# A message-passing network over sorted edges: the read-back pass moved into layer 0, and PE's addresses worked out at the front of a step

## The chip, the cores and the metric

The kernel runs on one core of one Trainium2 chip. The metric is the device time of one launch, in microseconds (us). Engines are named as in the profile: PE does the matrix products, DVE, ACT and POOL do elementwise work, SP issues transfers (DMA), and every engine has a sequencer that fetches instructions, does its register work and waits for semaphores; the rows call it PEldq, SPq, POOLq.

## The reference

A graph of 3125 nodes with 64 features and 100000 edges sorted by destination, each with 16 attributes and one of 4 types. Three message steps, three relation layers, and a layernorm behind each half:

```python
# three times, with h = x at first
msg_in = concatenate([h[src], h[dst], edge_attr], axis=1)      # 100000 x 144
msg = silu(msg_in @ W1e + b1e) @ W2e + b2e
agg = segment_sum(msg, dst) / max(deg, 1)
h = h + silu(concatenate([h, agg], axis=1) @ W1n + b1n) @ W2n + b2n
x = layernorm(x + h)
# three times, with h = x at first; relu behind the first two
seg = edge_type * n_nodes + dst
agg = segment_sum(h[src], seg) / max(cnt, 1)                    # one mean for each node and type
h = h @ root + b + einsum('rni,rio->no', agg.reshape(4, n_nodes, 64), W)
x = layernorm(x + h)
```

## The kernel before

**Stages.** Nodes stand in 25 blocks of 128. A first stage (to about 1331 us) counts the edges by pair of blocks, gives every edge a slot, and scatters one record of 68 floats per edge to `recs` in DRAM: 64 with the edge's share of the message MLP, and four more, SRCLOC and PLACE (the local row of the source and of the destination), TYPE and PT (place and type in one number). Slots are in tiles of 128 records; a tile has one pair of source blocks. There are 1280 tiles in NG = 160 groups of GT = 8. Then come six layers over all groups, `l` = 0 to 2 the message steps and 3 to 5 the relation layers.

**The read-back pass** (L417 to L430 on SP, L668 to L675 on ACT, L875 to L883 on PE) stands between them. For each of the 160 groups SP loads its records, ACT copies their last four columns into `meta_t`, and SP may load again when a buffer of four is read. Then PE turns the columns SRCLOC and PLACE into rows, 20 transposes, ACT copies these, and SP stores them to `rows_d`. Layer 0 starts when this is stored.

**A group in layer 0.** SP loads the rows of the group, the same for all 128 partitions (`load_rows`, L433 to L437, two buffers `row_in`), and its records (`load_records`, L438 to L446, four buffers `rec_in`). DVE compares the rows with the partition's number, which gives three one-hot matrices for 8 tiles (`transposed_hots`, L1315 and L1316). They serve PE as gathers (`gather_tile`: per tile three products, L934, L935, L938, with parts of a table that holds the node terms in three bf16 parts), are turned for the sums (L948), and are stored to `hots_d` (`store_hots`, L451), from which layers 1 to 5 load them. DVE adds the gathered parts to the record (`messages`, L1337 and L1341, with the types' compare L1329), ACT does two silus (L701, L702), POOL splits the result in three bf16 parts with ACT's help (L537, L540, L707), PE sums it over the edges (`sum_messages`, L968, LAG = 3 groups later), ACT copies the sums out (L714) and POOL adds them to the block's total (L552 to L562). In layers 1 and 2 the one-hots come by DMA (`load_hots`), and the rest is the same.

**A group in layers 3 to 5.** PE gathers with two products a tile (L934, L935) and does 32 products of sums by type (L977), four behind each gathered tile. DVE makes the one-hots for those (`type_hots`, L1357) from a column of `meta_t`.

**Places.** Which 192 columns of the table a tile reads depends on the data: `load_places` (L913 to L918) loads the 8 offsets of the next group, in layers 0 to 2 the destination's offset too, from `places` in SBUF into registers of PE's sequencer. `stage` (L982 to L1011) takes a snapshot of the registers (L988, L990), waits for the one-hots, and works out each address just ahead of its product. In layers 0 to 2 `load_places(g + 1)` stands behind the sums, at the step's end; in layers 3 to 5 in mid-step, behind the fourth tile.

**What sets the order.** The program is written out by hand. Each engine has one stream, four groups a loop pass, and waits for the others' semaphores; a semaphore is counted up once for each group, `done(n)` being group n's count. On SP a step of layer 0 is: load rows k, load records k, store one-hots k - 2. On ACT it is keep_hots (L693), middle (L707), keep_msums (L714), messages (L701). On DVE it is the one-hots of the next group, then the additions of this one.

## Time and profile before

| what | value |
|---|---|
| time, median of 3 runs | 5863.55 us (5863.24 to 5865.77) |
| the profiled execution: its time, its span | 5864.59 us, 5862.9 us |
| mean granted clock of TensorE | 0.863 |
| PE busy | 4725.5 us (81%), 47638 instructions |
| PE's weight loads busy | 4058.5 us (69%) |
| DVE busy | 3972.5 us (68%), 9658 instructions |
| POOL busy | 3395.9 us (58%) |
| ACT busy | 2755.2 us (47%) |
| DMA | 975.41 MB in 358467 packets, mean 166 GB/s |
| chain that ended last | PE 56%, POOL 15%, issue 10%, DMA 9%, DVE 7% |

The shares are averages over stages that have different limits, so they say little about one change; the rows below are read stage by stage. The chain is followed back from the last instruction to whatever released each step; "issue" is time in which an engine waited for nothing that the profile shows. The ends of products on PE are modelled (a product shows some 0.25 us busy while they start 0.08 us apart), so PE's pace is read from the starts. The stages by time: first stage to 1331 us, read-back pass to 1511, layer 0 from 1516 to 2312, layers 1 and 2 with their node steps to about 3750, layers 3 to 5 to the end.

### The profile page before, as it was taken

The numbers are of one execution on the slowest core, as the hardware profiler recorded it, in microseconds if no ns is written. First come the engines' busy times: TensorE is split into PE (matmuls) and PEld (weight loads), VectorE is DVE, ScalarE is ACT, GpSimd is POOL, SyncE is SP. The second block draws the span as 40 slices with busy tenths as digits, with TensorE's granted clock in tenths as the row PEclk, the third lists the DMA queues.
The fourth block names the chain that finished last, engine by engine and source line by source line (L and its number), as shares of the span: only waits on it lengthen the run. The fifth ranks groups of instructions, "written<-read, shape, count | busy, mean of one in ns | idle before, by whom it ended". The sixth has DMA issues, their size and how long they took to land.

```text
span 5862.9 us, 173813 instructions
## 1 busy us (share of the span) xinstructions
PE 4725.5 (81%) x47638; PEld 4058.5 (69%) x47639; DVE 3972.5 (68%) x9658; ACT 2755.2 (47%) x4407; POOL 3395.9 (58%) x4499
## 2 busy tenths in 40 slices
PE   2666666660577777888888888899999999999998
PEld 2444444440466665777767777699998999999997
DVE  6444444440589997777767777688875888578885
ACT  1111111112456665677757777555554555455553
POOL 0777777770367775455535555366653666446663
PEclk9755555555799999999999999899998999899997
DMA  8111111117899997777757777244432444234441
GB/s 327 29 29 29 29 29 29 29 28 244 272 312 333 334 334 245 248 264 266 264 176 265 263 265 265 92 133 133 132 120 83 132 132 133 93 109 133 132 133 58
DMA packets 358467, 975.41 MB, mean 166 GB/s; under 512 B 71168, under 2 KB 83796, under 8 KB 358411
## 3 DMA queue, kind: packets, MB, share of 16 engines
q1 hardware_dynamic: 317352, 946.00, 48.9%
q0 software_dynamic: 38400, 28.13, 2.7%
q10 hardware_dynamic: 2658, 0.51, 0.0%
q8 instruction: 37, 0.61, 0.0%
q14 instruction: 20, 0.16, 0.0%
HBM read 774.54 MB, written 199.06 MB: 166 GB/s over the span
## 4 chain that ended last, share of the span: by engine, by line
PE 56%; POOL 15%; issue 10%; DMA 9%; DVE 7%; another core or an unknown queue 2%; ACT 1%; DVEq 0%; POOLq 0%; SPq 0%; ACTq 0%
PE sums L977 21%; POOL recs L517 14%; PE gat L934 10%; PE gat L935 10%; DMA arena<-rows_d 5%; PE gat L938 4%; PE sums L968 4%; DMA arena<-recs 3%; PE sums L948 2%; DMA recs<-arena 2%; DVE arena L1341 1%; PE gat L1060 1%; DVE arena L1316 1%; DVE arena L1337 1%
## 5 line engine op out<-in xcount | busy, mean ns | idle before, releaser
L934 PE MATMUL gat<-table,arena 128*128 x7680 | 1913.4, 249 | 370.8 <-DVE arena L1341 186.7
L935 PE MATMUL gat<-table,arena 128*128 x7680 | 1916.7, 250 | 0.0
L977 PE MATMUL sums<-arena 128*128 128x192 bf16 x15360 | 1887.2, 246 | 0.0
L1357 DVE TENSOR_SCALAR arena<-iota_s,meta_t 128x512 bf16<-128x512 int16 x3840 | 1523.0, 469 | 363.2 <-PE sums L977 363.2
L977 PEld LDWEIGHTS sums<-arena 128*128 128x128 bf16 x15360 | 1325.3, 98 | 0.1
L517 POOL DMA_INDIRECT recs<-arena x800 | 949.8, 1187 | 377.4 <-issue 374.9
L721 ACT CAST arena<-gat 128x768 bf16<-128x768 f32 x960 | 767.0, 799 | 809.3 <-PE gat L935 809.3
L934 PEld LDWEIGHTS gat<-table,arena 128*128 128x128 bf16 x7680 | 747.7, 97 | 548.3 <-issue 482.1
L938 PE MATMUL gat<-table,arena 128*128 x3840 | 959.9, 250 | 0.0
L540 POOL TENSOR_TENSOR arena<-arena 128x512 bf16<-128x512 f32 x480 | 532.6, 1110 | 726.3 <-ACT arena L707 726.0
L1341 DVE TENSOR_TENSOR arena<-arena,gat 128x256 f32<-128x256 f32 x1920 | 812.0, 423 | 65.8
L935 PEld LDWEIGHTS gat<-table,arena 128*128 128x128 bf16 x7680 | 748.0, 97 | 137.2 <-issue 0.4
L592 POOL TENSOR_TENSOR arena<-arena 128x256 f32<-128x256 f32 x480 | 414.5, 864 | 656.7 <-ACT arena L729 655.9
L693 ACT COPY arena<-sums 128x1024 bf16<-128x1024 bf16 x480 | 486.3, 1013 | 518.2 <-PE sums L948 517.8
L1337 DVE TENSOR_TENSOR arena<-gat,arena 128x256 f32<-128x256 f32 x960 | 402.8, 420 | 263.4 <-PE gat L938 262.1
L832 PE MATMUL gat<-arena 25*125 25x39 bf16 x800 | 232.0, 290 | 401.8 <-DVE arena L1179 401.8
L656 ACT COPY arena<-gat 25x1000 bf16<-25x1000 bf16 x100 | 98.4, 984 | 829.8 <-PE gat L806 807.8
L832 PEld LDWEIGHTS gat<-arena 25*125 25x125 bf16 x800 | 141.2, 176 | 445.9 <-DVE arena L1179 429.7
L598 POOL TENSOR_TENSOR arena<-arena 128x256 f32 x480 | 384.6, 801 | 91.2 <-POOL arena L595 91.2
L968 PE MATMUL sums<-arena 128*128 128x192 bf16 (+1 forms) x3840 | 406.1, 248 | 11.1 <-ACT arena L714 10.9
L729 ACT COPY arena<-sums 128x768 f32<-128x768 f32 x480 | 386.2, 804 | 9.9 <-PE sums L977 9.9
L938 PEld LDWEIGHTS gat<-table,arena 128*128 128x128 bf16 x3840 | 380.3, 99 | 13.4
(184 smaller groups left out, 6228.6 us busy)
## 6 DMA issues: line engine op xcount, KB each, us to landing
arena<-hots_d SPq DMA_DIRECT2D x320, 768.0 KB, 4.5
arena<-hots_d SPq DMA_DIRECT2D x480, 512.0 KB, 3.5
arena<-recs SPq DMA_DIRECT2D x640, 272.0 KB, 3.9
hots_d<-arena SPq DMA_DIRECT2D x160, 768.0 KB, 8.1
arena<-rows_d SPq DMA_DIRECT2D x160, 512.0 KB, 6.9
recs<-arena SPq DMA_DIRECT2D x1, 43520.0 KB, 119.4
recs<-arena POOLq DMA_INDIRECT x800, 2.9
arena<-in_edge_attr_dram SPq DMA_DIRECT2D x100, 62.5 KB
```

What stands on the lines that cost most here:

```text
L517: pool.indirect_dma_start(recs, bass.IndirectOffsetOnAxis(ap=addr_out[s][:, j:j + 1].bitcast(U32), axis=0), rec_out[s][:, j, :], None).the ...
L540: pool.tensor_tensor(parts[u][:, :, 2 * HID:K3], left[s], parts[u][:, :, HID:2 * HID], ALU.subtract).then_inc(low_made, 1)
L693: act.copy(oh[u], oh_ps[u % 2].rearrange("p (j n) -> p j n", n=P)).then_inc(hot_out, 1)
L721: act.copy(gb[u % 4][:, 4 * h:4 * h + 4, :], gat[:, 1024 * h:1024 * h + 1024].rearrange("p (j w) -> p j w", j=4) [:, :, 0:K3]).then_inc(ga ...
L934: pe.matmul(at, ohT[u][:, 0, tile], table_flat[:, bass.ds(off[j], K3)], start=True, stop=False)
L935: ins = pe.matmul(at, ohT[u][:, 1, tile], table_next[:, bass.ds(off[j], K3)], start=False, stop=l >= LAYERS)
L938: ins = pe.matmul(at, ohT[u][:, 2, tile], table_flat[:, bass.ds(dst_off, K3)], start=False, stop=True)
L968: ins = pe.matmul(accp[u % 2][:, 0:w], oh[u][:, j, :], parts[u][:, j, 0:w], start=j == 0, stop=j == GT - 1)
L977: ins = pe.matmul(accp[s][:, 256 * r:256 * r + K3], oh4[u][:, t, r * P:(r + 1) * P], gb[u][:, t, :], start=t == 0, stop=t == GT - 1)
L1337: dve.tensor_tensor(z[s][:, tiles, :], found_parts[:, tiles, 0:HID], rec[:, tiles, 0:HID], ALU.add).then_inc(z_step, 1)
L1341: ins = dve.tensor_tensor(z[s][:, tiles, :], z[s][:, tiles, :], found_parts[:, tiles, m * HID:(m + 1) * HID], ALU.add)
L1357: ins = dve.tensor_scalar(oh4[u][:, j, :], iota_s[:], meta_t[:, bass.ds(GT * g + j, 1), PT - HID], None, ALU.is_equal)
```

## The change

- **The read-back pass is gone.** In layer 0 SP loads each group's records six groups ahead (`load_first`, eight buffers `rec_in` in place of four). PE turns their columns SRCLOC and PLACE into 8 rows each, two transposes a group, four groups ahead (`turn_rows`); ACT copies them to `rows_sb` (`keep_rows`, three groups ahead), SP stores them to `rows_d` (`store_rows`, three ahead), waits for that store, and loads them for all partitions (`load_rows`, two ahead). `rows_d` now has the 16 rows of a group side by side, so that a partition reads 4 KB in one piece.
- **`meta_t` is replaced by `place_type`**, one column in place of four, which ACT copies from the records of each group in layer 0 (`keep_types`) and DVE reads in layers 3 to 5.
- **Loops.** Layer 0 runs eight groups a loop pass on every engine, the other layers four as before. The number of groups stays 160.
- **The front of a step on PE**, in all six layers: behind the snapshot, the addresses of all the step's products are worked out at once (`lower_ap`), and in layers 0 to 2 `load_places(g + 1)` follows there, ahead of the wait for the one-hots, in place of standing behind the sums.
- POOL's wait ahead of layer 0 is for the scatters themselves.

```diff
-    NG += -NG % 4
+    NG += -NG % 8
...
-    rows_d = nc.dram_tensor("rows_d", [2, NT, P], BF16, kind="Internal").ap()
+    rows_d = nc.dram_tensor("rows_d", [NG, 2 * GT, P], BF16, kind="Internal").ap()
...
+    rows_by_group = rows_d.rearrange("g (m j) p -> j g m p", m=2)
+    rows_flat = rows_d.rearrange("g r p -> g (r p)")
 
...
-        meta_t = sb("meta_t", [P, NT, 4])
+        place_type = sb("place_type", [P, NT])
...
-            with sp.Fori(0, QUADS) as i:
-                for u in range(4):
-                    sp.wait_ge(meta_kept, done(4 * i + u - 4))
-                    sp.dma_start(rec_in[u].rearrange("p j w -> p (j w)"),
-                                 recs_by_group[:, bass.ds(4 * i + u, 1), :].rearrange("p a w -> p (a w)")
-                                 ).then_inc(meta_loaded[u], 16)
-            sp.wait_ge(rows_cast, TP // 2)
-            for m in range(2):
-                sp.dma_start(rows_d[m].rearrange("(c q) p -> q c p", q=P), rows_sb[:, m, :, :]
-                             ).then_inc(rows_stored, 16)
-            sp.wait_ge(meta_kept, done(NG - 1))
-            sp.wait_ge(rows_stored, 32)
-
-            def load_rows(k, u):
+            def load_first(k, u):
+
+                if not isinstance(k, int) or k >= 8:
+                    sp.wait_ge(gat_read, done(2 * (k - 8) + 1))
+                    sp.sem_inc(recs_go, 1)
+                    sp.wait_ge(type_kept, done(k - 8))
+                sp.dma_start(rec_in[u].rearrange("p j w -> p (j w)"),
+                             recs_by_group[:, bass.ds(k, 1), :].rearrange("p a w -> p (a w)")
+                             ).then_inc(rec_loaded[u], 16)
+
+            def store_rows(k, u):
+
+                sp.wait_ge(rows_cast, k + 1)
+                sp.sem_inc(rows_go, 1)
+                sp.dma_start(rows_by_group[:, bass.ds(k, 1), :, :].rearrange("j a m p -> j (a m) p"), rows_sb[u % 2]
+                             ).then_inc(rows_stored[u % 2], 16)
+
+            def load_rows(k, u, i):
+                sp.wait_ge(rows_stored[u % 2], 16 * (k // 2 + 1) if isinstance(k, int) else 64 * i + 16 * (u // 2 + 1))
+                sp.sem_inc(rows_go, 1)
                 sp.wait_ge(ohT_made, done(k - 2))
                 sp.sem_inc(rows_go, 1)
-                sp.dma_start(row_in[u % 2], rows_by_group[:, bass.ds(k, 1), :].rearrange("m a e -> a m e")
-                             .to_broadcast([P, 2, GT * P])).then_inc(rows_loaded[u % 2], 16)
+                sp.dma_start(row_in[u % 2].rearrange("p m e -> p (m e)"),
+                             rows_flat[bass.ds(k, 1), :].to_broadcast([P, 2 * GT * P])).then_inc(rows_loaded[u % 2], 16)
...
+            def first_layer(k, u, i):
+                known = isinstance(k, int)
+                if not known or k + 6 < NG:
+                    load_first(k + 6, (u + 6) % 8)
+                if not known or k + 3 < NG:
+                    store_rows(k + 3, u + 3)
+                if not known or k + 2 < NG:
+                    load_rows(k + 2, u + 2, i)
+                if not known or k >= 1:
+                    store_hots(k - 1, u + 7)
+
+            for k in range(6):
+                load_first(k, k)
+            for k in range(3):
+                store_rows(k, k)
+            for k in range(2):
+                load_rows(k, k, 0)
+            for k in range(8):
+                first_layer(k, k, 0)
+            with sp.Fori(1, OCTS - 1) as i:
+                for u in range(8):
+                    first_layer(8 * i + u, u, i)
+            for k in range(NG - 8, NG):
+                first_layer(k, k % 8, 0)
+            store_hots(NG - 1, 3)
...
+            def keep_rows(k, u, i):
+                act.wait_ge(rows_turned, k + 1)
+                act.wait_ge(summed, done(k - 7))
+                if not isinstance(k, int):
+                    act.wait_ge(rows_stored[u % 2], 64 * i + 16 * (u // 2))
+                elif k >= 2:
+                    act.wait_ge(rows_stored[u % 2], 16 * (k // 2))
+                act.copy(rows_sb[u % 2], rows_ps[(u + 1) % 2]).then_inc(rows_cast, 1)
+
+            def keep_types(k, u, i):
+                act.wait_ge(rec_loaded[u % 8], 16 * (k // 8 + 1) if isinstance(k, int) else 16 * i + 16)
+                act.copy(place_type[:, bass.ds(GT * k, GT)], rec_in[u % 8][:, :, PT]).then_inc(type_kept, 1)
...
+                    def group(g, u, i, l=l):
+                        known = isinstance(g, int)
+                        if l == 0 and (not known or g + 3 < NG):
+                            keep_rows(g + 3, u + 3, i)
+                        keep_hots(g, u % 4)
+                        if not known or g >= 1:
+                            middle(g - 1, (u + 3) % 4)
+                        if not known or g >= 4:
+                            keep_msums(g - 4, u % 4)
+                        if l == 0:
+                            keep_types(g, u, i)
+                        messages(g, u % 4)
+
...
-            pe.wait_ge(meta_kept, done(NG - 1))
-            for r in range(TP // 2):
-                if r >= 4:
-                    pe.wait_ge(rows_cast, r - 3)
-                for a in range(4):
-                    m, c = divmod(4 * r + a, TP)
-                    ins = pe.transpose(work[r % 4][:, a * P:(a + 1) * P], meta_t[:, c * P:(c + 1) * P, m], ident[:])
+            def turn_rows(k, u, i):
+
+                pe.wait_ge(rec_loaded[u % 8], 16 * (k // 8 + 1) if isinstance(k, int) else 16 * i + 16 * (1 + u // 8))
+                if not isinstance(k, int) or k >= 2:
+                    pe.wait_ge(rows_cast, k - 1)
+                pe.wait_ge(acc_read, done(k - 9))
+                for m in range(2):
+                    ins = pe.transpose(rows_ps[(u + 1) % 2][:, m, :], rec_in[u % 8][:, :, SRCLOC + m], ident[:])
                 ins.then_inc(rows_turned, 1)
...
                         off = [pe.snap(r, min_val=0, max_val=SPAN * ROWW * (NS - 1)) for r in tile_regs[u % 2]]
                         if l < LAYERS:
                             dst_off = pe.snap(dst_reg[u % 2], min_val=0, max_val=ROWW * (NB - 1) + K3)
+                            pe.lower_ap(table_flat[:, bass.ds(dst_off, K3)])
+                        for r in off:
+                            pe.lower_ap(table_flat[:, bass.ds(r, K3)])
+                            pe.lower_ap(table_next[:, bass.ds(r, K3)])
+                        if l < LAYERS:
+                            load_places(g + 1, u + 1)
                         gather_ready(g, u, i)
                     if l < LAYERS:
                         if gathers:
                             for j in range(GT):
                                 gather_tile(g, u, j, off, dst_off)
-                            turn_dst_hots(g, u)
+                            turn_dst_hots(g, u % 4)
+                        if l == 0 and (not known or g + 4 < NG):
+                            turn_rows(g + 4, u + 4, i)
                         if not known or g >= LAG:
                             sum_messages(g - LAG, (u + 4 - LAG) % 4)
-                        if gathers:
-                            load_places(g + 1, u + 1)
...
-                    stage(g, g, 0)
-                with pe.Fori(1, QUADS) as i:
-                    for u in range(4):
-                        stage(4 * i + u, u, i)
+                if l == 0:
+                    for k in range(4):
+                        turn_rows(k, k, 0)
+                    for g in range(8):
+                        stage(g, g, 0)
+                    with pe.Fori(1, OCTS - 1) as i:
+                        for u in range(8):
+                            stage(8 * i + u, u, i)
+                    for g in range(NG - 8, NG):
+                        stage(g, g % 8, 0)
...
                         ins = dve.tensor_scalar(oh4[u][:, j, :], iota_s[:],
-                                                meta_t[:, bass.ds(GT * g + j, 1), PT - HID], None, ALU.is_equal)
+                                                place_type[:, bass.ds(GT * g + j, 1)], None, ALU.is_equal)
```

How this moves instructions shows in three places. First PE, layer 1, from the sums that end a step to the first gathers of the next; "ISA" is register work of the sequencer (snapshot, addresses). Before:

```order
L968 MATMUL sums<-arena 128x192 [waits low_made,hot_out]
L968 MATMUL sums<-arena 128x192 x7
L916 ISA
L916 TENSOR_LOAD places
L988 ISA
L931 ISA [waits hots_loaded1]
L934 ISA [waits gat_read]
L934 MATMUL gat<-table,arena 128x192
L935 ISA
L935 MATMUL gat<-table,arena 128x192
```
and now:

```order
L1012 MATMUL sums<-arena 128x192 [waits low_made,hot_out]
L1012 MATMUL sums<-arena 128x192 x7
L1032 ISA
L1035 ISA
L1038 ISA
L1037 ISA x2
L1038 ISA x3
L960 ISA
L960 TENSOR_LOAD places
L975 ISA [waits hots_loaded1]
L978 MATMUL gat<-table,arena 128x192 [waits gat_read]
L979 MATMUL gat<-table,arena 128x192
```
The load of places is now behind the snapshot (L1032) and behind the entries that work out the addresses (L1035 to L1038), and the entries between the gathers are gone.

Second PE in layer 3, between the last sums of one step and the first of the next. Before:

```order
L977 MATMUL sums<-arena 128x192 x4
L988 ISA
L931 ISA [waits hots_loaded1]
L934 ISA [waits gat_read]
L934 MATMUL gat<-table,arena 128x192
L935 ISA
L935 MATMUL gat<-table,arena 128x192
L954 REGISTER_ALU
L961 REGISTER_ALU [waits acc_read]
L977 MATMUL sums<-arena 128x192 [waits gat_read,oh_made]
```
and now:

```order
L1021 MATMUL sums<-arena 128x192 x4
L1032 ISA
L1037 ISA
L1038 ISA x3
L1037 ISA x2
L1038 ISA
L975 ISA [waits hots_loaded3]
L978 MATMUL gat<-table,arena 128x192 [waits gat_read]
L979 MATMUL gat<-table,arena 128x192
L998 REGISTER_ALU
L1005 REGISTER_ALU [waits acc_read]
L1021 MATMUL sums<-arena 128x192 [waits gat_read,oh_made]
```
Here no load of places moves; seven entries with all addresses (L1037, L1038) come between the snapshot and the wait for the one-hots, and those ahead of single gathers are gone.

Third SP, one group of layer 0. Before:

```order
L433 REGISTER_ALU
L435 ISA [waits ohT_made]
L435 DMA arena<-rows_d 128x2x1024
L440 ISA
L444 ISA [waits gat_read,types_made]
L444 DMA arena<-recs 128x544
L451 ISA [waits ohT_made]
L451 DMA hots_d<-arena 128x3072
```
and now (L429 loads records six groups ahead, L437 stores the rows of the group three ahead, L445 loads those of the group two ahead):

```order
L426 ISA
L429 ISA [waits gat_read,type_kept]
L429 DMA arena<-recs 128x544
L437 ISA [waits rows_cast]
L437 DMA rows_d<-arena 8x2x128
L443 REGISTER_ALU [waits rows_stored1]
L445 DMA arena<-rows_d 128x2048 [waits ohT_made]
L459 ISA [waits ohT_made]
L459 DMA hots_d<-arena 128x3072
```
The load of rows has moved behind two more waits, those for the cast rows and for their store, and the store of the one-hots is for the group before in place of the one two before.

## Rows read from the trace of the kernel before

**Rows 1.** The page's busy tenths in 40 equal slices, PE's row.
```profile
PE   2666666660577777888888888899999999999998
```

**Rows 2.** Chain of waits, 1325 to 1512 us: start, us, what.
```profile
1328.49 2.99 DMA recs<-arena
...
1333.72 3.67 DMA arena<-recs
...
1501.28 4.53 PE gat L881 x20
```

**Rows 3.** Timeline, 1495 to 1531 us: start, us, engine, line, operation, out<-in, [idle before].
```profile
1516.65 0.88 DVE L1315 TENSOR_SCALAR arena<-arena,lane 128x1024 bf16<-128x1024 bf16 x2 [192.99 <-DMA arena<-rows_d]
...
1527.55 0.88 DVE L1341 TENSOR_TENSOR arena<-arena,gat 128x256 f32<-128x256 f32 x2
...
1529.08 0.61 ACT L702 ACTIVATE arena<-arena 128x512 bf16<-128x512 f32 x1
```

**Rows 4.** Stages: us, then PE, PEld, DVE, ACT, POOL busy, PEclk, DMA share, GB/s.
```profile
1512.00:1762.00 250.00, 181.61 (x1879) 150.61 (x1880) 201.94 (x476) 138.17 (x231) 159.56 (x264) 0.92 0.94 307
1762.00:2312.00 550.00, 410.84 (x4524) 335.23 (x4522) 514.67 (x1132) 328.97 (x570) 395.45 (x698) 0.98 0.96 331
2350.00:3005.00 655.00, 572.40 (x6400) 463.63 (x6400) 494.19 (x1121) 457.28 (x800) 363.49 (x640) 0.99 0.78 260
```

**Rows 5.** Groups by line, layer 0 (1512 to 2312 us): busy, mean ns, idle before.
```profile
L1315 DVE TENSOR_SCALAR arena<-arena,lane 128x1024 bf16<-128x1024 bf16 x320 | 190.8, 638 | 237.2 <-DMA arena<-rows_d 233.6 <-issue 0.2
...
L714 ACT COPY arena<-sums 128x196 f32<-128x196 f32 x160 | 51.0, 319 | 3.2 <-POOL arena L562 3.2
```

**Rows 6.** DMA issues, 1505 to 1530 us: KB each, median us to landing.
```profile
rows_d<-arena SPq DMA_DIRECT2D x2, 320.0 KB, 3.5
```

**Rows 7.** DMA issues, layer 1, 2400 to 2800 us.
```profile
arena<-hots_d SPq DMA_DIRECT2D x99, 768.0 KB, 4.5
```

**Rows 8.** The load of rows, L435, by line, 1505 to 1600 us.
```profile
DMA to landing us min/median/max: 5.7/8.2/9.6
```

**Rows 9.** Timeline in layer 0, 2004 to 2007 us, DVE and SP.
```profile
2004.28 1.32 DVE L1316 TENSOR_SCALAR arena<-arena,lane 128x1024 bf16<-128x1024 bf16 x1
...
2005.85 0.39 SPq L435 DMA_DIRECT2D arena<-rows_d  x1
...
2006.67 0.33 SPq L444 DMA_DIRECT2D arena<-recs  x1
```

**Rows 10.** Timeline of PE in layer 1, 2599.9 to 2604.3 us.
```profile
2600.19 0.25 PE L934 MATMUL gat<-table,arena 128*128 x1 [0.38 <-issue]
...
2602.44 0.61 PE L948 MATMUL sums<-ident_b,arena 128*128 128x128 bf16 x8
2602.89 0.83 PE L968 MATMUL sums<-arena 128*128 128x192 bf16 x8
2603.97 0.25 PE L934 MATMUL gat<-table,arena 128*128 x1 [0.25 <-issue]
```

**Rows 11.** L916 on PE's sequencer, 2602 to 2604 us: min/median/max ns, starts.
```profile
L916 PEldq FUSED_REGOPS  x1: 65/65/65, 2602.5 to 2602.5; - x1
L916 PEldq TENSOR_LOAD <-places x1: 836/836/836, 2602.7 to 2602.7; - x1
```

**Rows 12.** The snapshot L988 in layer 3, 4005 to 4006 us.
```profile
L988 PEldq FUSED_REGOPS  x1: 150/150/150, 4005.4 to 4005.4; - x1
```

**Rows 13.** Timeline of PE in layer 3, 4006 to 4007.5 us.
```profile
4006.84 0.25 PE L934 MATMUL gat<-table,arena 128*128 x1
```

**Rows 14.** Sequencer entries of other lines: L582 in layer 3, others in layer 1.
```profile
L582 POOLq FUSED_REGOPS  x6: 84/84/84, 4010.4 to 4089.6; - x6
...
L1016 PEldq COMPARE_BRANCH  x24: 207/208/208, 2414.3 to 2784.6; - x24
...
L988 PEldq FUSED_REGOPS  x75: 165/165/165, 2402.7 to 2796.7; - x75
...
L934 PEldq FUSED_REGOPS  x796: 37/37/42, 2400.2 to 2799.1; - x199
```

More of the change, by code:

```diff
@@ L204, in gnn_kernel @@
         loops_at = at
-        for s in range(4):
+        for s in range(8):
             t, at = carve(at, GT * REC)
@@ L211, in gnn_kernel @@
         macc_v = macc.rearrange("p (b w) -> p b w", b=NB)
+        rows_sb = []
+        for s in range(2):
+            t, at = carve(at, P, BF16, GT)
+            rows_sb.append(t.rearrange("j (m p) -> j m p", m=2))
         rings_at = at
@@ L267, in gnn_kernel @@
         oh_ps = [sums[:, 1024 * s + 512:1024 * s + 1024].bitcast(BF16) for s in range(2)]
+        rows_ps = [sums[0:GT, 1024 * s + 256:1024 * s + 512].rearrange("j (m p) -> j m p", m=2) for s in range(2)]
         hot_turned = gat[:, 0:512].bitcast(BF16)
@@ L347, in gnn_kernel @@
         stored = sem("stored")
-        rec_loaded = [sem(f"rec_loaded{s}") for s in range(4)]
+        rec_loaded = [sem(f"rec_loaded{s}") for s in range(8)]
         rows_loaded = [sem(f"rows_loaded{s}") for s in range(2)]
@@ L519, in _ @@
                             rec_out[s][:, j, :], None).then_inc(rec_stored[s], 16)
-            pool.wait_ge(meta_kept, done(NG - 1))
+            for s in range(2):
+                pool.wait_ge(rec_stored[s], 16 * GT * (EG // 2))
             pool.wait_ge(tables_in, 32)
```

113 lines of the change are left out of this document (50 added, 63 removed).

## The prediction

> **What bounds the kernel now.** I read the busy table by slices first, then the busy time of each engine by stage, then the chain of waits stage by stage, and last single steps in the timeline. PE's row of slices shows three regimes: a hole in the tenth slice, sevens and eights, then nines [rows 1]. The hole is the pass that the change takes away. The chain goes from the last scatter of records from 1333.72 through 160 loads of records to 20 transposes at 1501.28 [rows 2], then through the store of the rows and their first load; nothing else runs, and the first one-hot compare of layer 0 starts at 1516.65 [rows 3]. The scatter landed at 1328.49 + 2.99 = 1331.48, so the pass and the start after it cost 185.2 us.
>
> Layer 0 runs 160 groups from 1516.65 to 2312, 795 us, or 4.97 a group. DVE is busy (201.9 + 514.7)/160 = 4.48 of that, and the DMA rings 0.94 to 0.96 of the time [rows 4]. DVE sat idle 233.6 us before its first compare, waiting for the rows [rows 5]. So this layer has two masters: a loop "rows land, one-hots are made, the next load into that buffer starts", and DVE itself. In layers 1 and 2 PE sets the pace: 6400 matmuls in 655 us, 40 a group, 4.09 us a group [rows 4]. In layers 3 to 5 it runs back to back, 48 matmuls a group: the nines at the end of its row [rows 1].
>
> **The pass goes.** What starts layer 0 now is a chain for group 0 alone: load of records 3.7 [rows 2], two transposes and a copy about 1.1, store of its rows 3.5 [rows 6], load of rows 5.7 [rows 8], issues between them 1.3, and 1.6 for standing among five more loads of records: 16.9 us in place of 185.2. That is **-168**.
>
> **The loop of the row loads gets longer.** Before, the load of rows k+2 starts 0.25 us after the one-hots of k are done: L1316 ends at 2005.60, the issue is at 2005.85 [rows 9]. In the changed order on SP it stands behind the store of rows k+3. That waits for ACT's copy of rows k+3, which stands on ACT behind the messages of group k-1. These wait for DVE's additions of group k-1, and on DVE those come after the one-hots of k, which wait for rows k. So from landing k to issue k+2:
> - DVE, one-hots of k and additions of k-1: 4.4 (4.48 on average; a little less when POOL is less busy);
> - ACT, two silus: from 1528.43 (1527.55 + 0.88) to 1529.69, 1.26 [rows 3];
> - the copy of 256 columns with its waits, 0.42 (196 columns take 0.32 [rows 5]);
> - SP: 0.25 to the issue of the store, and 0.82 from that to the next issue with its two waits, as between the issues at 2005.85 and 2006.67 [rows 9]: 1.07.
>
> Together 7.15 us. Then the load lands after L. The loop spans two groups, since there are two row buffers, so a group takes (7.15 + L)/2. L is 5.7 at least, 8.2 at the median when DMA is full [rows 8]. After the change DMA has gaps (4.97 of work in more than 6 us), and a row of 4 KB in place of two of 2 KB may help; 768 KB landed in 4.5 where the rings were 0.78 busy [rows 4, 7]. I take 5.3, which gives 6.22 a group. Bounds: 3.9 gives 5.5 a group, 7.3 gives 7.2. The cost is (6.22 - 4.97) x 160 = **+200**; the bounds are +90 and +360. The additions on PE (two transposes of 4.53/20 = 0.23 [rows 2]) and ACT (a copy of 8 columns, less than 0.32) fall into time that this loop leaves idle, and cost nothing; if the loop were shorter than 5 us they would be late next. Bytes are the same but for 4 KB a group.
>
> By the Trainium skill ("DMA: Bandwidth & Descriptors", section "Anatomy of one DMA") a transfer takes about 2 us plus its bytes over 436 GB/s, 3.2 us for these 512 KB. The trace has 5.7 for the first one, with almost nothing ahead of it; by the rule the layer would cost 168 us less.
>
> **The front of the step on PE, layers 1 and 2.** PE's sequencer handles register work in order, and what it has sent ahead to PE hides it. Before, at a plain step: the address of the places at 2602.5 (65 ns), a load of nine registers 836 ns, then one entry of 165 ns and two short ones like the 37 ns of L934 [rows 10, 11, 14]. With 0.06 between entries that is the 1.45 us from there to the gather at 2603.97. At 2602.5 PE had 5 of its 8 transposes and all 8 sums before it; the last sum started near 2603.47, half a us before the next gather. Now the same stretch holds the snapshot (165 ns), seven entries of about six operations, the address and the load of places, and the wait. An entry of six operations takes 84 ns on POOL [rows 14]. So 0.22 + 7 x 0.14 + 0.12 + 0.90 + 0.10 + 0.03 = 2.35 us.
>
> How far ahead can the sequencer be? In layer 3 the snapshot starts at 4005.4, and the next step's first gather on PE at 4006.84 - 0.08 for the weight load: 1.4 us, 17 matmuls of 0.082 [rows 12, 13]. It could send faster: a tile's entries take it 0.25 us, its six matmuls 0.49. So this lead is a cap. In layers 1 and 2 the last 17 matmuls are 8 sums of 0.082, 8 transposes of 0.056 and one gather: 1.18 us. So 2.35 - 1.18 = 1.17 stay open. In return the gathers run without register entries, at 0.082: 24 x 0.082 + 8 x 0.056 + 8 x 0.082 = 3.07, in place of 3.3. A plain step becomes 4.24; before it was 3.78 (2600.19 to 2603.97) [rows 10]. Every fourth carries the branch (208 ns [rows 14], its counter and gaps) and one more entry, 0.12 a group on average; filling the layer adds 0.05. So 4.41 against 4.09: 320 groups, **+102**. The bounds: nothing of the front visible, and the next limit is the ring DVE additions, two silus, DVE's remainder, 3.5 us: -0.5 a group, -160; a load that is as slow as in layer 0 would give +0.5 more, which I think not likely here.
>
> **Layers 3 to 5.** The load of places stays in mid-step. The front is the snapshot, six such entries, a shorter one and the wait: 0.22 + 6 x 0.14 + 0.10 + 0.10 + 0.03 = 1.29 us against a lead of 1.39, so it is just covered. Behind it stand three waits of 0.09 each between the first gathers (0.165 of work) and the first sums, with no lead left: 0.05 open. At the branch the front is 1.68, so 0.29 + 0.15 are open. On average 0.14 a group, 480 groups: **+68**. Bounds: 0, and 0.35 a group (+170).
>
> **Sum.** -168 + 200 + 102 + 68 = +202 on the profiled execution's 5864.59 (its span of 5862.9 and 1.7 around it); the median of the runs is 5863.55, 1 us away. Forecast 6067 us.
>
> **Rivals.**
> - *The sequencer's lead is longer than I read it* (ends faster). If it covers 2.35 us in layers 1 and 2, PE loses nothing there, and a group drops to about 3.6 us: -0.45 x 320 = -144, layers 3 to 5 at 0. Sum -168 + 200 - 144 = -112: 5753. For it: in layers 1 and 2 no step shows more than 13 matmuls sent, so no cap was met there. Against it: the constant 1.4 us in layer 3 [rows 12, 13]. It decides from 2.35 us of lead, twice what I see. The Trainium skill ("TensorE: Matmul & The Clock Gate", "Architectural detail") gives TensorE a queue of 64; counted as 32 weight loads with their matmuls it would reach far enough in those layers. The trace stops at 17.
> - *The rows land quickly* (L 3.9, fronts as forecast): 5.5 a group, -168 + 90 + 102 + 68 = +92: 5957.
> - *The front costs and gives nothing*, the loop as forecast: +32: 5897.
> - *The change doesn't lengthen the loop*, because ACT's copy is ready earlier than I read: layer 0 keeps 4.97, -168 + 170 = +2: 5867. Against it is the order on ACT, which is fixed.
>
> **How the numbers follow.** Forecast 0.50 (own range 5990 to 6200), longer lead 0.17, quick rows 0.15, neutral front 0.10, unchanged loop 0.08. What a measurement of this kernel can tell from no change is 0.2%, 12 us. Slower: 0.50 + 0.15, 0.08 of the neutral front and 0.02 of the unchanged loop, 0.75. Faster: 0.17, 0.02 of the neutral front and 0.03 of the unchanged loop, 0.22. Same: the rest of the unchanged loop, 0.03. The range 5800 to 6240 leaves out the longer lead for the most part, and the tail above.
>
> **What would show each step.** The first one-hot compare near 1348. In layer 0, a group near 6.2 us, with the load of rows issued about 1 us after ACT's copy and DVE idle some 1.7 us a group before its first compare, waiting for rows. In layers 1 and 2, 4.4 us a group, gathers 0.082 apart, and a hole of about 1.2 us on PE before each step's first gather, put down to issue. In layers 3 to 5, a hole of 0.3 to 0.4 at every fourth step. I am wrong if layers 1 and 2 take under 3.9 a group, or if the loads of rows are issued before ACT's silus of their step.

## The result

The changed kernel takes 6041.06 us (median of 4 runs, 6040.43 to 6042.81) against 5864.45 in the same comparison: a ratio of 1.0302, 95% interval 1.0284 to 1.0319. The profiled execution has a span of 6039.2 us against 5862.9, so 176.3 us are to be explained; its mean granted clock is 0.862 against 0.863, so the clock is not the reason. Single executions of two kernels below were over 1.5% longer than the fastest of the same kernel (6110.9 against 5978.1 us with the front alone, 5714.4 against 5496.0 us with the last combination), and the ratios leave them out. The stages, from the starts of the first one-hot compare and of the first and last gather of each layer in both traces ("a group" is the time from first to last gather over 160):

| stage | before us | after us | difference | forecast |
|---|---|---|---|---|
| first one-hot of layer 0 at | 1516.65 | 1344.99 | -171.7 | -168 |
| layer 0, from there to its last gather (a group) | 778.7 (4.86) | 1007.7 (6.29) | +229.0 | +200 |
| layer 1, first to last gather (a group) | 641.6 (4.010) | 677.6 (4.235) | +36.0 | +51 |
| layer 2 | 641.5 | 678.1 | +36.6 | +51 |
| layer 3 (a group) | 631.4 (3.946) | 644.3 (4.027) | +12.9 | +23 |
| layer 4, layer 5 | 631.2, 631.4 | 643.9, 643.8 | +12.7, +12.4 | +45 |
| between and behind the layers | 390.5 | 398.8 | +8.3 | 0 |
| sum | | | +176.3 | +202 |

The page of the changed kernel, PE's slices [rows 1] and, below them, the granted clock and the DMA share:

```profile
PE   2666666656666666777777777799999999999998
...
PEclk9555555568888887999999999899997999899997
DMA  8111111127777775777747777344442444334441
```

The hole in PE's tenth slice is gone. Layer 0 now fills eight slices (the ninth to the sixteenth), a five and seven sixes where five sevens stood, and DMA, nines before in layer 0, shows sevens. The first compare, in the timeline, answers to [rows 3]:

```profile
1344.99 0.88 DVE L1376 TENSOR_SCALAR arena<-arena,lane 128x1024 bf16<-128x1024 bf16 x2 [20.23 <-DMA arena<-rows_d]
```

The stages, layer 0 in two and layer 1, answer to [rows 4] (us, then PE, PEld, DVE, ACT, POOL busy, PEclk, DMA share, GB/s):

```profile
1345.00:1595.00 250.00, 162.31 (x1614) 148.80 (x1614) 170.77 (x393) 123.23 (x264) 126.31 (x211) 0.87 0.73 246
1595.00:2350.00 755.00, 499.01 (x5022) 454.93 (x5023) 536.22 (x1197) 386.70 (x837) 418.12 (x716) 0.89 0.75 253
2415.00:3085.00 670.00, 514.38 (x6294) 478.78 (x6293) 481.14 (x1105) 457.00 (x785) 311.95 (x616) 1.00 0.74 250
```

In layer 0 every engine is less busy than in [rows 4], DMA too: no engine is full, so a loop of waits must set the pace. The compare of the rows by form, layer 0, for [rows 5]:

```profile
L1376 DVE TENSOR_SCALAR arena<-arena,lane 128x1024 bf16<-128x1024 bf16 x320 | 202.6, 673 | 282.2 <-DMA arena<-rows_d 282.2
```

and the load of rows from issue to landing, by line, for [rows 8]:

```profile
DMA to landing us min/median/max: 4.2/5.7/6.3
```

DVE waits 282.2 us for rows, of which 20.23 lie ahead of the first compare. Before it was 233.6, of which 192.99 lay ahead of the first: the wait within the layer went from 41 to 262 us. Two groups of layer 0 in the timeline show the loop, for [rows 9]:

```profile
1904.13 0.61 ACT L727 ACTIVATE arena<-arena 128x512 bf16<-128x512 f32 x1
...
1904.65 0.34 ACT L697 CAST arena<-sums 8x256 bf16<-8x256 f32 x1
...
1904.95 1.71 DVE L1376 TENSOR_SCALAR arena<-arena,lane 128x1024 bf16<-128x1024 bf16 x2 [1.39 <-DMA arena<-rows_d]
...
1905.26 0.31 SPq L437 DMA_DIRECT2D rows_d<-arena  x1
...
1906.07 0.35 SPq L445 DMA_DIRECT2D arena<-rows_d  x1
...
1906.59 0.47 DVE L1377 TENSOR_SCALAR arena<-arena,lane 128x1024 bf16<-128x1024 bf16 x1
...
1910.48 0.63 ACT L727 ACTIVATE arena<-arena 128x512 bf16<-128x512 f32 x1
1911.00 0.34 ACT L697 CAST arena<-sums 8x256 bf16<-8x256 f32 x1
...
1911.58 0.31 SPq L437 DMA_DIRECT2D rows_d<-arena  x1
...
1912.21 0.35 SPq L445 DMA_DIRECT2D arena<-rows_d  x1
```

The second silu (L727) ends at 1904.74, the cast of the rows (L697) at 1904.99, the store (L437) is issued at 1905.26 and the load of rows (L445) 0.81 later. The one-hots of group k start at 1904.95 with the landing of its rows; the load for k + 2 is issued at 1912.21, 7.26 us later, though its buffer was read at 1907.06. PE in layer 1, timeline, for [rows 10]:

```profile
2600.15 0.61 PE L992 MATMUL sums<-ident_b,arena 128*128 128x128 bf16 x8
2600.60 0.83 PE L1012 MATMUL sums<-arena 128*128 128x192 bf16 x8
2602.31 0.25 PE L978 MATMUL gat<-table,arena 128*128 x1 [0.88 <-issue]
...
2604.30 0.61 PE L992 MATMUL sums<-ident_b,arena 128*128 128x128 bf16 x8
2604.75 0.83 PE L1012 MATMUL sums<-arena 128*128 128x192 bf16 x8
2606.48 0.25 PE L978 MATMUL gat<-table,arena 128*128 x1 [0.90 <-issue]
```

The load of places there, by line (min/median/max ns), for [rows 11]:

```profile
L960 PEldq FUSED_REGOPS  x1: 60/60/60, 2601.2 to 2601.2; - x1
L960 PEldq TENSOR_LOAD <-places x1: 841/841/841, 2601.3 to 2601.3; - x1
```

and the packed entries of the addresses (L1038), by line, for [rows 14]:

```profile
L1038 PEldq FUSED_REGOPS  x280: 74/74/74, 2502.3 to 2796.8; - x140
```

Gathers come 0.082 apart now (24 of them from 2602.31 to 2604.30), and ahead of the first there is a hole that the profile puts down to issue. The snapshot, which starts at 2600.01, and what is behind it take until 2602.31. Counted over the trace, 17 products start between a snapshot (L1032) and the first gather that comes of it, at 587 of 590 snapshots in layers 1 to 5, and never more. In layer 3 only the step with the branch has holes; in the timeline of PE, for [rows 13]:

```profile
4106.56 0.49 PE L1021 MATMUL sums<-arena 128*128 128x192 bf16 x4
4107.06 0.25 PE L978 MATMUL gat<-table,arena 128*128 x1
4107.15 0.25 PE L979 MATMUL gat<-table,arena 128*128 x1
4107.38 0.42 PE L1021 MATMUL sums<-arena 128*128 128x192 bf16 x3
```

The four sums from 4106.56 should be followed by the gather at 4106.89; it comes 0.17 late, and the sum at 4107.38 another 0.15. Before the change no two starts in layers 3 to 5 are over 0.083 apart, their first 20 and last 5 us left out.

### The profile page after: what moved, and what is told of

The parts are those of the page before. It is cut to its first block, busy times and chain, and to the rows that moved or that the text cites. A ratio compares the mean times of both kernels' runs of the same rounds, so it can differ in the third digit from the quotient of the medians.

```text
span 6039.2 us, 164954 instructions
## 1 busy us (share of the span) xinstructions
PE 4743.4 (79%) x47938; PEld 4219.4 (70%) x47939; DVE 3961.0 (66%) x9658; ACT 2783.2 (46%) x4562; POOL 3312.6 (55%) x4499
## 4 chain that ended last, share of the span: by engine, by line
PE 52%; DVE 9%; issue 7%; DMA 7%; ACT 2%; POOL 1%; SPq 1%; DVEq 0%; POOLq 0%; ACTq 0%
PE sums L1021 21%; PE gat L978 10%; PE gat L979 9%; DMA arena<-rows_d 6%; PE gat L982 3%; DVE arena L1406 3%; PE sums L1012 3%; PE sums L992 2%; DVE arena L1402 2%; PE gat L1121 1%; DVE arena L1415 1%; PE gat L1119 1%; ACT arena L727 1%; DVE arena L1377 1%; DVE arena L1376 1%
## 5 line engine op out<-in xcount | busy, mean ns | idle before, releaser
L978 PE MATMUL gat<-table,arena 128*128 x7680 | 1940.3, 253 | 691.0 <-issue 370.1
L979 PE MATMUL gat<-table,arena 128*128 x7680 | 1937.6, 253 | 0.0
L1422 DVE TENSOR_SCALAR arena<-iota_s,place_type 128x512 bf16<-128x512 int16 x3840 | 1523.7, 469 | 403.1 <-PE sums L1021 403.1
L978 PEld LDWEIGHTS gat<-table,arena 128*128 128x128 bf16 x7680 | 770.0, 100 | 832.9 <-issue 482.9
L982 PE MATMUL gat<-table,arena 128*128 x3840 | 990.8, 258 | 0.0
L979 PEld LDWEIGHTS gat<-table,arena 128*128 128x128 bf16 x7680 | 772.2, 101 | 3.7
L982 PEld LDWEIGHTS gat<-table,arena 128*128 128x128 bf16 x3840 | 395.8, 103 | 3.7
```

The costliest lines, as they stand in the source:

```text
L978: pe.matmul(at, ohT[u % 4][:, 0, tile], table_flat[:, bass.ds(off[j], K3)], start=True, stop=False)
L979: ins = pe.matmul(at, ohT[u % 4][:, 1, tile], table_next[:, bass.ds(off[j], K3)], start=False, stop=l >= LAYERS)
L982: ins = pe.matmul(at, ohT[u % 4][:, 2, tile], table_flat[:, bass.ds(dst_off, K3)], start=False, stop=True)
L1422: ins = dve.tensor_scalar(oh4[u][:, j, :], iota_s[:], place_type[:, bass.ds(GT * g + j, 1)], None, ALU.is_equal)
```

## Experiments

Twelve kernels in three sets. "us a group" is again the time from first to last gather of a layer in the profiled execution, over 160.

**The front alone.** The kernel before, with `lower_ap` for all addresses and `load_places` behind the snapshot, as in the second hunk of the change:

```diff
+                            pe.lower_ap(table_flat[:, bass.ds(dst_off, K3)])
+                        for r in off:
+                            pe.lower_ap(table_flat[:, bass.ds(r, K3)])
+                            pe.lower_ap(table_next[:, bass.ds(r, K3)])
+                        if l < LAYERS:
+                            load_places(g + 1, u + 1)
...
-                        if gathers:
-                            load_places(g + 1, u + 1)
```


> The kernel before with nothing changed but the front of the step on PE, in all six layers (addresses worked out at once, the load of places ahead of the wait for the one-hots). Theory (the front is register work that the sequencer can hide only behind 17 matmuls): layers 1 and 2 go from 4.01 to 4.24 us a group, layers 3 to 5 from 3.946 to 4.025, as in the changed kernel, +73 and +38; layer 0 keeps its time, since DVE and the rows set its pace. About 5864 + 111 = 5975. Rival (the layers 1 to 5 became slower through the other edits, such as the narrower column for the type compare or the records' buffers): within 10 us of 5864. Second rival: the front also shows in layer 0, up to +50 more, 6025.

Measured: 4.235 us a group in layers 1 and 2, 4.02 to 4.05 in layers 3 to 5, within 0.003 of the changed kernel but for layer 3 with 4.047. Its times spread: 5978.1, 5980.5, 6042.3 and 6110.9, ratio 1.0241 (1.0185 to 1.0297). The lower two agree with 5975, the mean of the lower three is 6000. The profiled execution is the longest, with 906 us in layer 0 against 778 before; there DVE waits 106.6 us for gathers in 122 groups, which is the second rival's picture. The executions do not agree on it, so what the front costs in layer 0 of this kernel, and why one execution pays it and another does not, stays open. That the front makes layers 1 to 5 slower is shown.

**The front taken out.** The changed kernel with those lines the other way round, in all layers.

> The changed kernel with PE's front of the step put back as it was before in all six layers; the read-back in layer 0 stays. Theory: layers 1 to 5 return to 4.01 and 3.946 us a group, layer 0 stays at 6.29: 6041 - 111 = 5930. Rival (a part of layer 0's loss is PE's longer front): layer 0 at 5.9 or less, below 5870.

Measured: 5896.47 us, ratio 1.0066 (1.0049 to 1.0083). Layers 1 to 5 are back at 4.01 and 3.945. Layer 0 went to 985.6 us, 22 less than in the changed kernel: the front has a price in layer 0 that I had set at nothing, though a tenth of the layer's loss and not the rival's part. 207 us remain there with the read-back and SP's order alone, where I forecast 200.

**Two issues exchanged on SP.**

```diff
+                if not known or k + 2 < NG:
+                    load_rows(k + 2, u + 2, i)
                 if not known or k + 3 < NG:
                     store_rows(k + 3, u + 3)
-                if not known or k + 2 < NG:
-                    load_rows(k + 2, u + 2, i)
```


> The changed kernel with two issues on SP exchanged in layer 0: the load of rows k+2 ahead of the store of rows k+3. Theory (the loop of two row buffers runs through the additions, the silus and the cast because the load stands behind the store): that loop is cut. What is left is the store itself, which now has to land before the load of the next step: one-hots k done, 2.6 additions, 1.26 silus, 0.42 copy, 0.25 issue, 3.5 landing, 0.3 issue, 5.3 landing over three groups, 1.8 for the one-hots, 15.4 over three groups: 5.1 us a group, 6041 - 185 = 5856. Rival (the time from issue to landing of the rows, or DMA traffic as such, sets layer 0): 6.2 to 6.3 us a group, 6041 within 15 us.

Measured: 5854.74 us, ratio 0.9991 (0.9981 to 1.0001), layer 0 at 5.126 us a group. So 186 us of layer 0's loss hang on this order: the loop is shown. The number was hit by luck, for the wrong reason. Groups by line on DVE, 1400 to 2100 us:

```profile
L1377 DVE TENSOR_SCALAR arena<-arena,lane 128x1024 bf16<-128x1024 bf16 x136 | 161.1, 1185 | 0.0
...
L1376 DVE TENSOR_SCALAR arena<-arena,lane 128x1024 bf16<-128x1024 bf16 x272 | 136.6, 544 | 5.7 <-issue 4.2 <-DMA arena<-rows_d 1.6
...
L1402 DVE TENSOR_TENSOR arena<-gat,arena 128x256 f32<-128x256 f32 x272 | 114.8, 422 | 34.8 <-PE gat L982 31.7
```

DVE hardly waits for rows any more (1.6 us in 136 groups); it would if the store's landing were the limit. It is busy 4.7 us a group and waits for gathers (31.7), which points to the front of the step; the last combination below tries that.

**One more group of lead.** The exchange, and 7, 5, 4 and 4 groups of lead in place of 6, 4, 3 and 3 for the load of records, the turn, the cast and the store.

> As the kernel with the two issues exchanged, and turning, casting, storing and loading of records each one group further ahead (5, 4, 4 and 7 groups). Theory: the store has a whole group more to land, and layer 0 is at the pace that it had before or a little better, 4.5 to 4.9 us a group (DVE is busy 4.48 of it): 6041 - 229 to - 285, 5756 to 5812. If it is no faster than with the exchange alone, the store's landing was not what was left.

Measured: 5925.22 us, ratio 1.0112 (1.0095 to 1.0129), 5.54 us a group: slower by 70 than the exchange alone, a miss. DVE waits for rows again, by the same view (DVE's line numbers are one higher in this kernel and the next, so L1377 here is the pair of compares that was L1376):

```profile
L1377 DVE TENSOR_SCALAR arena<-arena,lane 128x1024 bf16<-128x1024 bf16 x252 | 147.4, 626 | 126.7 <-DMA arena<-rows_d 126.3 <-issue 0.2
...
L1403 DVE TENSOR_TENSOR arena<-gat,arena 128x256 f32<-128x256 f32 x250 | 104.0, 416 | 7.0 <-PE gat L983 7.0
```

With 8 buffers and 7 groups of lead the load of records waits for the additions of the group before, and the load of rows stood behind it. The next kernel tests that.

```diff
+                if not known or k + 2 < NG:
+                    load_rows(k + 2, u + 2, i)
                 if not known or k + 7 < NG:
                     load_first(k + 7, (u + 7) % 8)
-                if not known or k + 2 < NG:
-                    load_rows(k + 2, u + 2, i)
```


> As the kernel with the two issues exchanged and all read-back work one group further ahead, and with the load of rows k+2 as the first issue of the step, ahead of the load of records k+7 too. Theory of why the one without this came to 5.54 us a group: with a lead of 7 groups over 8 buffers the load of records k+7 waits for the additions and the type copy of group k-1, and the load of rows stood behind that wait. Then layer 0 falls to DVE's pace with its contention, 4.71 us busy a group: 4.75 to 5.0 a group, 5785 to 5830 in all. Rival (the longer lead itself costs, by DMA or by the copies on ACT): 5.4 us a group or more, 5900.

Measured: 5896.25 us, ratio 1.0059 (1.0042 to 1.0076), 5.37 us a group.

```profile
L1377 DVE TENSOR_SCALAR arena<-arena,lane 128x1024 bf16<-128x1024 bf16 x256 | 126.6, 537 | 4.2 <-issue 3.9 <-DMA arena<-rows_d 0.2
...
L1403 DVE TENSOR_TENSOR arena<-gat,arena 128x256 f32<-128x256 f32 x258 | 108.8, 422 | 82.1 <-PE gat L983 81.1
```

The wait for rows went from 126.3 to 0.2 us, so its cause is shown; the time followed only in part, since DVE now waits 81.1 us for gathers. The longer lead bought nothing: 5.37 us a group against 5.126 without it, as the rival had it. Why it makes the gathers later was not tried.

**The load of places in mid-step.** The changed kernel:

```diff
-                        if l < LAYERS:
-                            load_places(g + 1, u + 1)
...
                                 gather_tile(g, u, j, off, dst_off)
+                                if j == 3:
+                                    load_places(g + 1, u + 1)
```


> The changed kernel with one edit: in layers 0 to 2 the load of places for the next group stands behind the fourth gathered tile, where it stands in layers 3 to 5, and not at the front of the step. All addresses are still worked out at the front. Theory (a front of 2.30 us against a lead of 1.25 leaves the hole of 1.05; the load with its address is 1.0 of it): the hole in layers 1 and 2 all but closes, the load is hidden behind the gathers, and the next limit is DVE's ring with the silus, about 3.5 us a group in place of 4.24: -235. Layer 0 gives back the 22 us that the front cost it. 6041 - 257 = 5784. Rival (the hole is set by something else that comes with the step, such as the one-hots' landing or the wait for DVE): layers 1 and 2 stay at 4.2, about 6020.

Measured: 5759.97 us, ratio 0.9832 (0.9816 to 0.9848). Layers 1 and 2 at 3.45 us a group: with the load gone from the front, a group is 0.79 us shorter, and the layers are faster than before the change. PE in layer 1:

```profile
2603.96 0.25 PE L982 MATMUL gat<-table,arena 128*128 x1
2604.28 0.25 PE L978 MATMUL gat<-table,arena 128*128 x1
...
2605.28 0.61 PE L992 MATMUL sums<-ident_b,arena 128*128 128x128 bf16 x8
2605.72 0.83 PE L1012 MATMUL sums<-arena 128*128 128x192 bf16 x8
2606.43 0.25 PE L978 MATMUL gat<-table,arena 128*128 x1
```

The hole ahead of the step is 0.05 us (the last sum ends its 0.082 at 2606.38), and behind the fourth tile 0.24 opens. A plain step is 3.29 to 3.38, one with the branch 3.77. Layer 0 gave back 28 us. Whether 3.45 is DVE's ring, as I had expected, is not shown.

The same place for the load, but each address ahead of its product:

> The changed kernel without any address worked out at the front, in all six layers (each is worked out ahead of its product, as before), and in layers 0 to 2 with the load of places behind the fourth gathered tile. Theory: the front is only the snapshot and the wait, the gathers of a step take 2.25 us in place of 1.97, and the load of 0.84 costs a little of the lead that is left: about 3.6 us a group in layers 1 and 2, -205; layers 3 to 5 back to 3.946, -38; layer 0 gives back 22. 6041 - 265 = 5776. If it is clearly faster or slower than the kernel with addresses in front and the load in mid-step, the packing of addresses has a price or a gain of its own in layers 1 and 2.

Measured: 5904.47 us, ratio 1.0075 (1.0058 to 1.0092): layers 1 and 2 at 4.012, where I had expected 3.6. PE, layer 1:

```profile
2602.17 0.25 PE L979 MATMUL gat<-table,arena 128*128 x1
2602.25 0.25 PE L982 MATMUL gat<-table,arena 128*128 x1
2603.21 0.25 PE L978 MATMUL gat<-table,arena 128*128 x1 [0.71 <-issue]
2603.34 0.25 PE L979 MATMUL gat<-table,arena 128*128 x1
```

The hole has only moved, behind the fourth tile. 4.012 is also the pace of the kernel before, with the load at the end. So in both it is the sequencer's whole work that sets the step, 4.0 us: 17 entries of addresses that start 0.12 us apart are 2.0, the load with its address 1.0, the snapshot 0.23, and the rest goes to waits and the branch. The trace of the kernel before bears this out: in the step from 2599.99 to 2603.77 no two entries of the sequencer have more than 0.1 us between them. Seven packed entries at 0.133 take 0.93. The gain needs the packing (4.012 without it, 3.45 with it, both with the load in mid-step), and the load behind it at the front was the loss. Packed addresses with the load at the step's end were not tried.

**Together.** First the load of rows first, the longer lead, and the plain addresses with the load in mid-step:

> The kernel with the load of rows first and the longer lead, together with the front put back and the load of places in mid-step in layers 0 to 2. The parts lie in different layers and should add: layer 0 4.75 to 5.0 us a group, layers 1 and 2 3.6, layers 3 to 5 3.946: 5787 - 205 - 38 = 5545 or a little more, some 5% below the kernel before.

Measured: 5706.41 us, ratio 0.9739 (0.9722 to 0.9755). 161 above the expectation: 132 are the 4.01 of layers 1 and 2 in place of 3.6, the rest is layer 0 at 4.93, where 5545 had stood for 4.75.

Then with packed addresses in layers 0 to 2 only, once with the longer lead, once with the changed kernel's leads and just the exchange:

> The last combination with one difference: in layers 0 to 2 the addresses are worked out at the front of the step and the load of places stands behind the fourth gathered tile (3.45 us a group in layers 1 and 2 with that, against 4.01 with each address ahead of its product); layers 3 to 5 keep the address ahead of each product (3.946). Theory: the parts add, layer 0 stays at DVE's and DMA's pace, 4.9 us a group: 5706 - 0.56 x 320 = 5527. Rival (the front costs in layer 0, where DVE waits for gathers): layer 0 at 5.1 or more, 5555 or more.

> As the last combination with the packed addresses, but with the leads of the changed kernel (6, 4, 3 and 3 groups) and only the two issues exchanged. Theory: the store of the rows must land within a step here, and it does at 5.1 us a group but not much below; layer 0 at 5.0 to 5.1, 5540 to 5560. If it is as fast as the kernel with longer leads, the exchange alone was all that the loop needed.

Measured: 5514.03 us, ratio 0.9404 (0.9389 to 0.9420), and 5497.15 us, ratio 0.9377 (0.9359 to 0.9396). Layer 0 at 4.84 and 4.74, layers 1 and 2 at 3.44, layers 3 to 5 at 3.946. The last kernel is the fastest. It disproves what I expected of the store: it keeps the short lead and is the faster one. It also shows what was left with the exchange alone, since in layer 0 it differs from that kernel only in the place of the load of places: DVE's wait for gathers is gone, and layer 0 went from 5.126 to 4.74 us a group. Its DVE in layer 0:

```profile
L1376 DVE TENSOR_SCALAR arena<-arena,lane 128x1024 bf16<-128x1024 bf16 x296 | 238.7, 846 | 15.5 <-DMA arena<-rows_d 11.4 <-issue 4.0
...
L1402 DVE TENSOR_TENSOR arena<-gat,arena 128x256 f32<-128x256 f32 x295 | 122.8, 416 | 0.0
```

**The front edit on the kernel before, done this way.**

> The kernel before with one edit: in layers 0 to 2 the addresses are worked out at the front of the step, and the load of places stands behind the fourth gathered tile. The read-back pass stays, layers 3 to 5 as before. Theory (in layers 1 and 2 PE's sequencer is the bound, and packed entries take it less time): 3.45 in place of 4.01 us a group, -180, layer 0 within 20 of its time: 5682. Rival (the gain belongs to the changed kernel's other edits): 5860.

Measured: 5688.49 us, ratio 0.9699 (0.9682 to 0.9715), 3.45 us a group in layers 1 and 2, layer 0 within 3 us of its time. The gain belongs to the packed addresses with the load in mid-step and needs nothing else of the change.

**Pieces of 2 KB in place of 4 KB.** The changed kernel with `rows_d` as [2, NT, P], and the load of rows with two pieces a partition.

> The changed kernel with the rows of a group in DRAM as in the kernel before: two pieces of 2 KB for a partition in place of one of 4 KB. All else, the order on SP too, as changed. Theory (half of the landing time goes into the group in layer 0, and larger pieces land faster): landing 6.2 or more in place of 5.6 us, layer 0 at 6.55 or more in place of 6.29 us a group, 6080 or more. Rival (the size of the pieces does not matter where DMA has gaps): 6041 within 10.

Measured: 6056.73 us, ratio 1.0331 (1.0314 to 1.0349); layer 0 at 6.378. DMA issues, 1400 to 2300 us (KB each, median us to landing), in it:

```profile
arena<-rows_d SPq DMA_DIRECT2D x140, 512.0 KB, 5.8
```

and in the changed kernel:

```profile
arena<-rows_d SPq DMA_DIRECT2D x142, 512.0 KB, 5.7
```

The landing differs by 0.1 us at the median and by 0.20 in the mean of all 160 loads (5.59 against 5.39), and half of that is the group's 0.09. There is an effect, some 14 us in layer 0, but a third of the 0.26 a group that I expected. So small pieces are not what made the landing 6.8 us in the kernel before (1600 to 2290 us); its rings were 0.96 busy there against 0.75, which is the likely reason and was not tried by itself.

## Why the prediction was right

By stage the forecast missed by -4 us (the pass), +29 (layer 0), -29 (layers 1 and 2), -30 (layers 3 to 5) and +8 (between the layers, where I had nothing; 3.9 of it lie behind layer 0, and I did not follow it). The mechanisms were right, but that the sum is off by no more than 26 us is partly luck: the misses of layer 0 and of layers 1 and 2 cancel.

**The pass** (-168, measured -171.7). The chain for one group took 12.4 us from the last scatter's landing (1332.57) to the first compare, where I had summed 16.9: the load of its records took 2.8 in place of 3.7, its rows landed in 4.1 in place of 5.7, and the 1.6 for standing among other loads did not show. The first stage ended 1.1 us later.

**The loop in layer 0** (+200, measured +229). From landing to issue I had 7.15, and the timeline shows 7.26 at one group, which is also the mean of the layer. Its parts were less well hit: at that group DVE takes 4.71 (forecast 4.4), the silus with the gap ahead of them 1.45 (1.26), the copy's rest 0.23 (0.42) and SP 0.87 (1.07), and the misses cancel. The landing is 5.7 at the median and 5.39 in the mean against 5.3. The exchange of two issues removes 186 us, so the named mechanism is shown and not argued. Of the 0.18 us a group that I missed, 0.07 are in the pace after (6.29 against 6.22) and 0.11 in the pace before: I took 795 us over 160, a window that runs past the last gather, and the pace was 4.86. Within +229, 22 are the front in this layer, which I had left at nothing since PE idles there. A misreading had no effect: the 233.6 us of [rows 5] are DVE's waits for rows in the whole layer, 192.99 of them ahead of the first compare, and not all ahead of it.

**Layers 1 and 2** (+102, measured +73). The hole is the front minus the lead, as forecast: front 2.30 (forecast 2.35), lead from the snapshot at 2600.01 to the end of the last sum at 2600.60 + 8 x 0.082 = 2601.26, 1.25 (forecast 1.18), a plain step 4.12 to 4.17 (forecast 4.24). The mis-sized term is the difference of the averages, 0.225 in place of 0.32: the group after the change is 4.235 and not 4.41, 0.12 of it from the plain step, while the 0.05 that I had added for filling the layer does not show; and 0.08 goes the other way, since I took 655 us over 160 as the pace before, and that window holds more than the steps. The pace was 4.01. That the kernel before was bound there by the sequencer's whole work I had not seen: I read its waits ahead of each step, not the sum of a step.

**Layers 3 to 5** (+68, measured +38). The branch opens 0.33 us every fourth step (forecast 0.44). The 0.05 in each of the other steps isn't there: the waits behind the front fit between the first products.

**The rivals.** The longer lead is refuted by the hole itself in layers 1 and 2. Quick rows: 5.7 at landing, 4.0 at the least in all of layer 0, against the 3.9 that it needed. The 3.2 us that I had beside it, from the Trainium skill ("DMA: Bandwidth & Descriptors", "Anatomy of one DMA"), stand there for transfers that GpSimd issues, while SP issues this one; no load of rows in layer 0 landed so fast. The unchanged loop and the neutral front are refuted by the exchange and by the front taken out. By the rule that I had put beside the first rival, a queue of 64 in the Trainium skill ("TensorE: Matmul & The Clock Gate", "Architectural detail"), the front would have been covered; the trace shows 17 products at nearly every step and never more.

## What to carry to other kernels

When a step is moved on a queue that issues in order, follow what it now stands behind through all engines until the loop closes, and divide by the number of buffers: that gave the sign and nearly the size here, and one exchanged pair of issues removed it. Register work packed into few entries takes the sequencer less time (0.93 us for seven entries in place of 2.0 for 17), but what stands in one piece at the front must be shorter than what the sequencer is ahead. When one long item goes from one place of a full sequencer to another, the hole goes with it; add up the sequencer's whole step first.

## What was not expected of the hardware

The load of nine registers takes 0.84 to 0.85 us in layers 1 and 2 wherever it stands, but in layer 0 its time differs from kernel to kernel. By line, min/median/max ns in layer 0, first at the step's end in the kernel before:

```profile
L916 PEldq TENSOR_LOAD <-places x158: 838/1331/3142, 1520.3 to 2286.2; - x158
```

at the front in the changed kernel:

```profile
L960 PEldq TENSOR_LOAD <-places x158: 836/2209/4509, 1350.1 to 2346.7; - x158
```

and at the step's end with the front taken out:

```profile
L960 PEldq TENSOR_LOAD <-places x153: 837/846/4188, 1352.7 to 2299.0; - x153
```

The place alone does not decide it, since the first and the third stand at the same place. Nor does the share of DMA: it is 0.75 to 0.76 in the second as in the third, and also during single loads the rings were 0.98 to 0.99 busy beside two of 0.84 and 0.86 us in the third kernel, and 0.94 to 1.02 beside three of 1.10 to 2.13 us in the second. What lengthens it stays open, and it was not tried by itself.

The third one-hot compare of 128x1024 took 1185 ns on average with the two issues exchanged and 622 in the changed kernel, the same instruction on the same data: 

```profile
L1377 DVE TENSOR_SCALAR arena<-arena,lane 128x1024 bf16<-128x1024 bf16 x160 | 99.5, 622 | 0.0
```

The traces show what stands beside it. With the exchange:

```profile
1907.47 1.17 POOL L562 TENSOR_TENSOR arena<-arena 128x512 bf16<-128x512 f32 x1 [1.26 <-ACT arena L732]
1907.61 1.31 DVE L1377 TENSOR_SCALAR arena<-arena,lane 128x1024 bf16<-128x1024 bf16 x1
```

In layer 0 of that kernel 127 of the 160 third compares take 1.3 us, and each of these ends 0.2 to 0.4 us behind a 128x512 instruction of POOL; the rest take 0.47 to 0.54. In the changed kernel 25 take 1.3 to 1.4 us, and the same holds for each. So the slow compares are those that run beside POOL's long instructions, and the order of work sets how many there are; no kernel was made that moves POOL alone. DVE is busy 4.43 us a group in the changed kernel and 4.69 with the exchange, for the same work.
